# Routing, the attention's tail and the expert scatters in another order

## What is computed

```python
x = x + attention(layernorm(x), ctx, ctx)   # 16 tiles of 128 tokens, width 128
x = x + moe(layernorm(x))

# attention: each token attends over its own 16 heads (head width 8, keys and values 64)
scores = einsum("blhk,blgk->blhg", Q_, K_) / sqrt(64)
x = softmax(scores) @ V_ ; x @ Wo + bo

# moe: 8 experts, the 2 best for each token, D 128, F 512
expert_gate, expert_index = top_k(softmax(x @ router_w), 2)
out = ((x @ (wv*sv)) * gelu(x @ (w*s))) @ (w1*s1)    # of the chosen experts
out = sum(expert_gate * out over the 2 choices)
```

## Time and profile before

| | us |
|---|---|
| median of 3 runs (lowest, highest) | 280.63 (280.06, 281.09) |
| the profiled execution | 278.34 |
| its span, first to last instruction | 276.6 |
| TensorE busy | 237.7 (86%) |
| VectorE busy | 178.0 (64%) |
| GpSimd busy | 151.9 (55%) |
| ScalarE busy | 118.5 (43%) |

### The profile page before, as it was taken

The page is one execution under the profiler, slowest core; times in us unless marked ns, Lnnn a source line. Parts: engine busy times, 40 slices in busy tenths (PEclk is TensorE's granted clock), DMA queues, the critical chain, the costliest instruction groups (busy, mean ns, idle before and its releaser), DMA issues.

```text
span 276.6 us, 6414 instructions
## 1 busy us (share of the span) xinstructions
PE 237.7 (86%) x1883; PEld 223.0 (81%) x1884; DVE 178.0 (64%) x475; ACT 118.5 (43%) x297; POOL 151.9 (55%) x160
## 2 busy tenths in 40 slices
PE   7997999979997999797996985999999999999500
PEld 7976888868886888696896974999999999999400
DVE  2799799877998789969174472454465455555216
ACT  2443422464544563326485242454465555554000
POOL 6956549754688859886545555253532423333300
PEclk9999999999999999979899899899999999999955
DMA  5979999995000100001200112312221121000058
GB/s 143 301 186 419 294 315 382 378 380 197 1 19 17 34 11 22 29 31 40 59 31 29 49 32 67 79 57 52 59 58 34 53 55 39 28 10 26 3 181 274
DMA packets 25518, 30.94 MB, mean 112 GB/s; under 512 B 2652, under 2 KB 16896, under 8 KB 25362
## 3 DMA queue, kind: packets, MB, share of 16 engines
q1 hardware_dynamic: 21708, 25.28, 29.1%
q0 software_dynamic: 2528, 4.77, 5.5%
q10 hardware_dynamic: 1254, 0.55, 0.7%
HBM read 16.26 MB, written 14.79 MB: 112 GB/s over the span
## 4 chain that ended last, share of the span: by engine, by line
PE 63%; DVE 11%; DMA 10%; POOL 5%; issue 5%; ACT 4%; SPq 1%; POOLq 0%; ACTq 0%; DVEq 0%
PE bank L976 20%; PE bank L995 10%; PE bank L899 9%; PE bank L856 8%; DMA routed<-rows,pos 6%; DVE qk L1114 3%; PE bank L783 3%; POOL routed L540 3%; DMA pv<-expert_out 2%; POOL pv L318 2%; PE bank L865 2%; ACT xn L600 2%; PE bank L907 2%; PE bank L909 2%; PE bank L908 2%
## 5 line engine op out<-in xcount | busy, mean ns | idle before, releaser
L561 POOL DMA_INDIRECT expert_out<-yo,xs x39 | 38.1, 978 | 59.1 <-DVE yo L1325 36.3
L318 POOL TENSOR_TENSOR pv<-probs,ctx_sb 128x1408 f32<-128x1408 f32 (+1 forms) x16 | 45.9, 2868 | 21.8 <-DVE probs L1168 18.9
L1316 DVE TENSOR_TENSOR hid<-bank,act_sb 128x512 f32<-128x512 f32 x39 | 26.9, 690 | 30.7 <-PE bank L976 16.0
L540 POOL DMA_INDIRECT routed<-rows,pos x32 | 35.0, 1093 | 21.1 <-DMA routed<-rows,pos 9.8
L995 PE MATMUL bank<-w_sb,hid 128*128 x312 | 43.1, 283 | 2.5 <-DVE yo L1325 2.4
L976 PE MATMUL bank<-xsT,g_tile 128*128 128x128 f32 x312 | 42.6, 280 | 1.1 <-issue 1.1
L995 PEld LDWEIGHTS bank<-w_sb,hid 128*128 128x128 f32 x312 | 39.4, 198 | 3.1 <-issue 3.1
L976 PE MATMUL bank<-xsT,v_tile 128*128 128x128 f32 x312 | 41.8, 277 | 0.0
L976 PEld LDWEIGHTS bank<-xsT,g_tile 128*128 128x128 f32 x312 | 39.1, 197 | 1.4 <-issue 1.3
L976 PEld LDWEIGHTS bank<-xsT,v_tile 128*128 128x128 f32 x312 | 38.5, 194 | 0.0
L1114 DVE TENSOR_TENSOR qk<-bank,ctx_ig 128x2048 f32<-128x2048 f32 x16 | 36.5, 2285 | 2.3 <-ACT ctx_ig L585 1.9
(11 more groups left out here) (171 smaller groups left out, 330.0 us busy)
## 6 DMA issues: line engine op xcount, KB each, us to landing
routed<-pad_rows SPq DMA_DIRECT2D x4, 2080.0 KB, 20.5
xs<-routed SPq DMA_DIRECT2D x39, 65.0 KB
g_sb<-in_L_ffn_w_dram SPq DMA_DIRECT2D x1, 2048.0 KB, 11.7
g_scale<-in_L_ffn_s_dram SPq DMA_DIRECT2D x1, 2048.0 KB, 16.3
v_sb<-in_L_ffn_wv_dram SPq DMA_DIRECT2D x1, 2048.0 KB, 28.0
pv<-expert_out SPq DMA_DIRECT2D x3, 512.0 KB, 4.9
x_sb<-in_x_dram SPq DMA_DIRECT2D x4, 256.0 KB, 6.2
ctx_sb<-in_ctx_dram SPq DMA_DIRECT2D x4, 256.0 KB, 6.3
```

The source lines that it names most:

```text
L318: return eng.tensor_tensor(pv[:, b, g0:g1, :, :], probs[:, b, :, g0:g1].rearrange("p h g -> p g h").unsqueeze(3).to_broadcast([P, many, H, ...
L540: pool.indirect_dma_start(out=routed[:, :], out_offset=bass.IndirectOffsetOnAxis(ap=pos[:, m % TOP, m // TOP:m // TOP + 1], axis=0), in_=r ...
L561: pool.indirect_dma_start(out=expert_out[:, :], out_offset=bass.IndirectOffsetOnAxis(ap=xs_i[:, t % XB, P:P + 1], axis=0), in_=yo[:, t % X ...
L1316: v.tensor_tensor(hid[:, c % 2, :], bank[3 + c % 2][:, :], act_sb[:, c % 2, :], ALU.mult).then_inc(hid_ready, 1)
```

## The change

The work is the same; its order differs at these places.

- Steps: GpSimd does `second_rstd` after `values` (was before). ScalarE does `normed` in the step after (lag `LOGITS`), behind the exponentials, where it was at the end of the step of lag `NORM`. Group 1's scatters go three, three, two over steps 10 to 12 (were two, three, three).
- The last tile's values: VectorE weights all 16 keys, GpSimd none (were 10 and 6).
- GpSimd's tail: four scatters of group 2 ahead of `second_rstd` of group 3 (was one), four behind; the wait for all of group 2 to land before group 3's first, and for all of group 3 before the first expert scatter (both new).
- Expert scatters: each of tiles 1 to 11 waits for the landing of the one before; from tile 12 there is no wait.
- The hand-written lists of ScalarE, TensorE and VectorE: see the diff. `places(2)` goes ahead of `value_sum(14)`, `products(0)` ahead of `value_sum(15)`; `choices(2)` ahead of `maximum(15)`, `positions(2)` ahead of the last values; `gates_in(2)` goes ahead of `residual(14)` and the table load, `residual(15)` behind `normed` of group 3's first three tiles, `gelu(2)` ahead of the last exponentials.

```diff
@@ -257,12 +257,11 @@
         POOL_KEYS = 11
         NORM, LOGITS, PLACES = 6, 7, 8
         EARLY_TABLE = EARLY_G * G + 3
-        LAST_POOL_KEYS = 6
 
 
         def sends(n):
 
-            return {9: 3, 10: 6, 11: G * TOP} if n < EARLY_G - 1 else {8: 2, 9: 5, 10: G * TOP}
+            return {9: 3, 10: 6, 11: G * TOP} if n < EARLY_G - 1 else {8: 3, 9: 6, 10: G * TOP}
 
 
         GATES_SCALED = (0, 0, 0, 0, 2, 1, 1, 2, 2)
@@ -320,6 +319,7 @@
                                      keys[:, g0:g1, :].unsqueeze(2).to_broadcast([P, many, H, HD]), ALU.mult)
 
         SENT = 16 * G * TOP
+        IN_A_ROW = 2
         full = (TILES - 3) // XB
         assert TILES - 3 == full * XB
 
@@ -500,8 +500,6 @@
 
                 def step(g, j):
 
-                    if a := group_at(g, j, NORM):
-                        second_rstd(a[0])
                     a = tile_at(g, j, 1)
                     if a and a[0] < NT - 1:
                         t, b = a
@@ -511,6 +509,8 @@
                         if second_on(t):
                             pool.wait_ge(zT_psum, t - 1)
                         values(pool, t, b, 0, POOL_KEYS).then_inc(pv_pool, 1)
+                    if a := group_at(g, j, NORM):
+                        second_rstd(a[0])
 
                     first, last = (sum(GATES_SCALED[n] for n in range(len(GATES_SCALED)) if n < AHEAD + G * g + j + d) for d in (0, 1))
                     for c in range(first, last):
@@ -535,7 +535,7 @@
                         pool.wait_ge(pos_ready, n + 2)
                     rows, pos = rows_of[last_group(n)], pos_of[last_group(n)]
                     for m in range(first, end):
-                        if n >= EARLY_G and m and m % 2 == 0:
+                        if n >= EARLY_G and m and m % IN_A_ROW == 0:
                             pool.wait_ge(scattered[n], 16 * m)
                         pool.indirect_dma_start(
                             out=routed[:, :],
@@ -545,19 +545,18 @@
 
                 for t in STEADY:
                     step(t // G, t % G)
-                pool.wait_ge(p_normed, NT)
-                pool.wait_ge(zT_psum, NT - 2)
-                values(pool, NT - 1, (NT - 1) % 2, 0, LAST_POOL_KEYS).then_inc(pv_pool, 1)
-                scatters(NG - 2, 0, 1)
+                scatters(NG - 2, 0, 4)
                 second_rstd(NG - 1, 0, G - 1, NG)
                 second_rstd(NG - 1, G - 1, G, NG + 1)
-                scatters(NG - 2, 1, G * TOP)
+                scatters(NG - 2, 4, G * TOP)
+                pool.wait_ge(scattered[NG - 2], SENT)
                 scatters(NG - 1, 0, G * TOP)
+                pool.wait_ge(scattered[NG - 1], SENT)
 
                 for t in range(TILES):
                     pool.wait_ge(yo_ready, t + 1)
-                    if t and t % 2 == 0:
-                        pool.wait_ge(y_sent[(t - 1) % XB], 16 * ((t - 1) // XB + 1))
+                    if 0 < t < XB:
+                        pool.wait_ge(y_sent[t - 1], 16)
                     pool.indirect_dma_start(
                         out=expert_out[:, :],
                         out_offset=bass.IndirectOffsetOnAxis(ap=xs_i[:, t % XB, P:P + 1], axis=0),
@@ -602,6 +601,8 @@
 
                     if a := tile_at(g, j, 1):
                         exponentials(a[0])
+                    if a := group_at(g, j, LOGITS):
+                        normed(a[0])
                     if a := tile_at(g, j, 0):
                         t, b = a
                         act.wait_ge(sT_psum, t + 1)
@@ -637,8 +638,6 @@
                     if a := tile_at(g, j, 2):
                         z_turned(a[0])
                         residual(a[0])
-                    if a := group_at(g, j, NORM):
-                        normed(a[0])
                     if a := group_at(g, j, PLACES):
                         gates_in(a[0])
 
@@ -734,32 +733,32 @@
 
                 for t in STEADY:
                     step(t // G, t % G)
-                exponentials(NT - 1)
                 logits_exponentials(NG - 2)
                 gate_weights(0, 0)
+                exponentials(NT - 1)
                 z_turned(NT - 2)
                 rows_but_gates(NG - 2)
+                gates_in(NG - 2)
                 residual(NT - 2)
                 rows_turned(0, 0)
                 load_gelu()
-                gates_in(NG - 2)
+                gelu(0, 0)
+                gate_weights(1, 1)
                 z_turned(NT - 1)
-                gate_weights(1, 1)
+                rows_turned(1, 1)
+                normed(NG - 1, 0, G - 1, NG)
                 residual(NT - 1)
-                rows_turned(1, 1)
-                gelu(0, 0)
-                normed(NG - 1, 0, G - 1, NG)
-                normed(NG - 1, G - 1, G, NG + 1)
                 gate_weights(2, 2)
                 gelu(1, 1)
+                normed(NG - 1, G - 1, G, NG + 1)
+                turned(NG - 1)
                 rows_turned(2, 2)
-                turned(NG - 1)
                 gate_weights(3, 3)
+                rows_but_gates(NG - 1)
                 rows_turned(3, 3)
-                rows_but_gates(NG - 1)
+                gelu(2, 2)
                 logits_exponentials(NG - 1)
                 load_gelu()
-                gelu(2, 2)
                 gates_in(NG - 1)
                 gate_weights(4, 4)
                 rows_turned(4, 4)
@@ -892,7 +891,8 @@
                         pe.wait_ge(sv_ready, 1)
                         pe.wait_ge(ld_bo, 16)
                     pe.wait_ge(pv_dve, t + 1)
-                    pe.wait_ge(pv_pool, t + 1)
+                    if t < NT - 1:
+                        pe.wait_ge(pv_pool, t + 1)
                     if first_on(t):
                         pe.wait_ge(x2_ready, t)
                     for key in range(H):
@@ -1006,14 +1006,14 @@
 
                 for t in STEADY:
                     step(t // G, t % G)
+                places(NG - 2)
                 value_sum(NT - 2)
-                places(NG - 2)
                 output_sum(NT - 2)
                 turn_rows(0, 0, 0)
+                products(0, 0)
                 value_sum(NT - 1)
                 turn_rows(1, 1, 0)
                 output_sum(NT - 1)
-                products(0, 0)
                 products(1, 1)
                 second_turn(NG - 1)
                 turn_rows(2, 2, 0)
@@ -1337,18 +1337,18 @@
                     step(t // G, t % G)
                 value_share(NT - 2)
                 value_weights(0, 0)
+                choices(NG - 2)
                 maximum(NT - 1)
-                choices(NG - 2)
                 normalise(NT - 1)
-                value_share(NT - 1, LAST_POOL_KEYS)
                 positions(NG - 2)
+                value_share(NT - 1, 0)
                 second_statistics(NT - 3)
                 second_statistics(NT - 2)
                 value_weights(1, 1)
-                second_statistics(NT - 1)
                 hidden(0, 0)
                 value_weights(2, 2)
                 left_table()
+                second_statistics(NT - 1)
                 hidden(1, 1)
                 value_weights(3, 3)
                 gated(0, 0)
```

## The result

The new kernel took 282.50 us in the median of four runs (280.66 to 284.46), the kernel before 280.86 beside it (280.06 to 283.86, four runs). The ratio is 1.0165, with a 95% interval of 1.0096 to 1.0233: slower, though by how much is less sure. The quotient of the two medians alone is 1.006, that of the two profiled executions (283.13 and 278.34, 4.8 us apart) 1.017; why the first is so much smaller isn't shown. On another chip the same kernel took 291.84 (289.39 to 293.31, four runs), ratio 1.0464 (1.0382 to 1.0547). The forecast was 281.3, with 0.27 for slower.

The account below looks back on a forecast made before the run. From 170 us TensorE is full, so group 3's first scatter and the end set the time: +2.4 there and -1.75 at the end give +0.65, 279.0 for a profiled run, 281.3 us as median; range 277.5 to 283.5.

Parts of the forecast that it names:

- the stretch from `qk(15)` to T0: From tile 15's `qk` to the start of group 2's first scatter (T0): 1.5 us shorter, T0 at 133.3.
- T0 to T3: From group 2's first scatter to the start of group 3's first (T3): 21.0 us instead of 19.0, +2.0.
- step 8: `normed` a step later, GpSimd's `values` first: `second_turn` ends at about 89.65 instead of 90.28, 0.63 us off.
- the table: Step 12, `second_rstd` behind `values(13)`: VectorE's `jumps` or `row_off` waits for GpSimd's `values`, +2.6 us.
- The third scatter: Step 10, three scatters of group 1 instead of two: `values(12)` and what follows up to `qk(15)` later, +1.4 us.
- The end: The last expert scatter no longer waits for the one before: -1.75 us, bounds -1 and -1.9.
- D: Rival: the last scatter gains nothing because two in flight hold each other up; 282.9 us, chance 0.07.
- B: Rival: the table isn't held in step 12, which takes the 2.6 off; 278.6 us, chance 0.25.
- rival C: TensorE stands before `places`, then `value_sum(14)` runs slow and T0 is 1.7 later; 283.0 us, chance 0.18.
- Hidden with 4.5 to spare: Expert scatters one by one: the twelfth lands at 206.3, the load that needs it (tile 23) is due at 211.
- E: Rival: TensorE stands less before tile 9 and keeps 2.4 GHz, saving a 1.7 us slow stretch; 279.6 us, chance 0.10.
- A: The forecast itself: 281.3 us, own range 279.9 to 282.7, chance 0.40.

Follow-up runs that it names:

- e15: e5 plus dummy TensorE matmuls, 22 ahead of its wait for `qk(15)` and 3 ahead of `picked`: 283.14 us, ratio 1.0073 to the kernel before.
- e3: The kernel before with only the new tail: all engines' lists behind the loop, four scatters first, wait for group 2. 281.48 us, ratio 1.013.
- e7: The new kernel with `second_rstd` ahead of `values` again in step 12 alone: 287.40 us, ratio 1.034 to the kernel before.
- e13: e7 with the expert scatters in pairs up to tile 12, then no wait: 279.95 us, ratio 0.996 to the kernel before.
- e10: e5 with `residual(15)` ahead of `normed` of group 3's first three tiles: 282.86 us, ratio 1.0138 to the kernel before.
- e14: The kernel before with expert scatters one by one up to tile 5, then no wait: 282.36 us, ratio 0.9961.
- e16: The kernel before with expert scatters one by one up to tile 7, then no wait: 285.24 us in one run, the kernel before 285.01.
- e17: The kernel before with expert scatters one by one up to tile 9, then no wait: 285.34 us in one run, the kernel before 285.01.
- e6: The kernel before with expert scatters in pairs up to tile 12, then no wait: 280.74 us, no ratio on record.
- e9: The kernel before with expert scatters one by one up to tile 11, then in pairs: 280.22 us, ratio 1.0052.
- e2: The kernel before with only group 1's scatters changed to three, three, two: 280.47 us, ratio 1.0062.
- e4: The kernel before with only the new expert scatter rule, tiles 1 to 11 one by one, then no wait: 285.09 us, ratio 1.0212.
- e1: The kernel before with only the new steps, `second_rstd` behind `values` and `normed` a step later: 281.45 us, ratio 1.0114.
- e5: The new kernel with the old expert scatters and without the wait for group 3: 284.20 us, ratio 1.0237 to the kernel before.
- e11: e5 plus dummy TensorE matmuls, 50 ahead of its wait for `qk(15)` and 8 ahead of `picked`: 288.08 us, ratio 1.03 to the kernel before.
- e18: The new kernel itself once more, on another chip: 291.84 us, ratio 1.0464 to the kernel before.

## Why the prediction was wrong, step by step

The forecast was a change of +0.65, close to nothing; the profile shows +4.24. The step that failed most is the stretch from `qk(15)` to T0: it was to give 1.5 and gave 0.11, because a value sum that I had put at 1.75 took 3.52. That is 1.4 of the 3.6 that are missing. The others are T0 to T3 (0.8), step 8 (0.6), the table (0.45) and the stretch behind tile 9's turn (0.9, less 0.4 ahead of it), which I had at nothing.

**Right.** What bounds the kernel: the move of T3 and the end account for all but 0.5 of the aligned 4.24. The stand in step 4, -1.45: measured -1.54 (VectorE's `qk` at 59.01 before and 57.95 after). The third scatter, +1.4: +1.33. The end, -1.75: -1.78. D didn't occur. Right too was that the table would be held, against B.

**The table was held by another operation and for longer.** I had looked for operations with two SBUF operands beside the values and found `jumps` and `row_off`. What is held is `w_off`, with one. The rule of the Trainium skill, "SBUF — State Buffer", section "Who interferes with whom", names for one input the copies, casts and `tensor_scalar`, which can contend in their two-port modes, and I had weighed only its other half. The trace agrees that these two kinds are held: `w_off` (TENSOR_SCALAR) ends 0.05 behind the values, and `v_tile` (COPY) takes 2.82 beside `values(14)` and 0.43 to 0.69 at all its other places. In which mode they ran, no run here shows. The price is 3.29 (3.46 less 0.17; small operations around it give 0.24 back), where I had 2.6: `w_off` began 0.57 ahead of the values and was held all the same.

**The gain in step 8 didn't arrive.** I had 0.63 there. At group 1's first scatter only 1.52 of the steps' 2.1 is left, which is step 4's share. `normed` starts at 87.37 there, where my working gives 86.68 on this scale (87.65 - 1.45 + 0.48), and stands 1.78 for GpSimd's `shift`; `second_turn` hangs on it, and the logits' first MAX8 comes 1.53 earlier (aligned), not 2.1. The timeline of the new kernel shows what is missing:

```profile
83.98 1.48 DVE L317 TENSOR_TENSOR pv<-probs,ctx_sb 128x640 f32<-128x640 f32 x1
84.70 0.81 POOL L493 TENSOR_TENSOR vtmp<-mv,eps 128x4 f32<-128x4 f32 x1
```

The four small operations of GpSimd that I had priced at 1.81 now lie beside VectorE's share, where `values` had lain before. The first took 0.81 instead of 0.21 and ended 0.05 behind that share (85.46), the third 0.37 instead of 0.19. It is the same in all eleven profiles with the new steps (0.79 to 0.81). So GpSimd is held by VectorE too, and I had counted the holding in one direction only.

**`qk(15)` to T0 was mis-sized: -1.5 forecast, -0.11 measured.** It is rival C. `places` ahead of `value_sum(14)` makes TensorE stand for `picked`, 0.65 us, and behind that the value sum takes 3.52 instead of 1.75; the other terms up to T0 are right within 0.3. e15 takes both slow stretches away and gets 1.8 back. e3's T0, on time with a value sum of 3.60, fits that too: the clock would cost there what `gates_in` ahead of the table load gives, but e3 doesn't part the two. I had put the point from which C decides at about 1 us of standing. That was no good measure: here the stand was 0.65, and in e7 and e13, behind the same stand of 0.64 and 0.65, `value_sum(14)` took 1.94. What decides between the two is not shown.

**T0 to T3: 21.8, 0.8 over what I took** and 0.2 over the upper bound, which held a slow stretch: it is there too, `products(1)` behind a stand of 3.98. e10 wins only 0.44 by moving that stretch. `gelu(2)` ahead of the two table loads, which I had at nothing on this path, has a small part: VectorE's gates are ready at 156.57, and ScalarE comes out of the loads to `gates_in` at 156.81. The rest isn't parted further.

**The expert scatters.** "Hidden with 4.5 to spare" held for the ring (though twelve scatters at 3.07 from 170.1 end at 206.9, not 206.3): in none of the twenty profiles does TensorE's turn of tile 10 or a later one wait for a load. It was the wrong question. I had costed each scatter by what waits for it and not by what twelve of them do when they are let go together. In the profile of the new kernel this costs nothing, on the other chip 8 us. On the latter the forecast misses by 10.5, and the largest part of that is this step.

**The rest.** From the turn of tile 9 to the last result there is 0.9 more than before, since TensorE stays at 1.2 GHz until 181 (granted clock 0.50 from 175.80 to 181.00; E, the other way round).

**The sum.** I had given A and B together 0.65, both at or under 281.3. Of the 3.6 that the profile is over the forecast, 3.1 lie ahead of T3: 1.0 at `qk(15)`, 1.4 up to T0, 0.8 up to T3.

## What to carry to other kernels

When an instruction of GpSimd with long SBUF operands is moved, list every VectorE instruction beside its new place, the small ones with one operand too: here one of nine columns was held for 3.3 us. List the small ones of GpSimd beside VectorE's long ones as well. An order in which TensorE waits for a short result ahead of a long sum should be costed at both clocks. And before a wait that paces DMAs is taken out, ask how large a backlog is let go there at once.

## What was not expected of the hardware

- **A burst of scatters mostly stops the other engines.** Six to twelve indirect scatters 1.27 us apart, each of 128 rows, went with 4 to 9 us, from within two us of their start, in which ScalarE, VectorE and TensorE began hardly any instruction, in six of seven profiles. The row of ScalarE says "remote". That it is the delivery of instructions is a guess: the transfers on the instruction queue don't sort the cases (e14, e16, e17 and the new kernel), and why the new kernel has no stand on one chip and one on another stays open.
- **A hidden slow stretch in the kernel before.** In step 4 TensorE stands 1.84 us ahead of tile 6's transposes. In five of nine profiles with the old steps they then took 1.91 us, in four (e6, e9, e16, e17) 3.24 to 3.57, and `qk(15)` came 1.6 to 1.7 later (in e9 2.9). Timeline of e9:

```profile
56.99 0.33 PE L844 MATMUL bank<-ident,xn 128*128 128x128 f32 x1 [1.84 <-ACT xn L600]
57.15 3.24 PE L856 MATMUL bank<-ident,qk 128*128 128x128 f32 x16
```

  With the new steps the stand is 0.30 and they took 1.91 in all eleven. So the steps may be worth more than in the profile that I had: 1.5 and, where the stretch is slow, an estimated 1.7 more (3.47 less 1.91, and what hangs on it). How often that is, these profiles don't say: those of one chip (e2, e3, e4) all have 1.91 and those of another (e16, e17) both the slow stretch, so it may go with the chip.
- **Held although it began first.** `w_off` began 0.57 or 0.58 ahead of GpSimd's values in all seven profiles with the fault (the new kernel, e1, e5, e10, e11, e15, e18), while a scatter was running, and ended with the values; in e7 it began just so beside a scatter and took 0.17. By the rule of the Trainium skill, "SBUF — State Buffer", section "Who interferes with whom", whoever issues first holds the ports: the trace shows the other order, and why stays open.
